# Bounded row gathers and spare blocks shared among the experts in a four-layer kernel

## The reference

```
router_logits = x @ gate_weight.T                       # 2048 x 32
top8 of softmax(router_logits), weights normalised
sec  -> the most similar of the 4 first choices, where the similarity is 0.5 or more
combine[token, expert] = sum of the weights that went there
for each expert:  y += (silu(x @ Wg.T) * (x @ Wu.T)) @ Wd.T * combine[:, expert]
out = layernorm(x + y)
```

## Time and profile before

| | |
|---|---|
| median of 3 runs | 1618.41 us (1615.53 to 1619.59) |
| the profiled execution | 1623.95 us |
| its span, first to last instruction | 1622.1 us |
| PE, DVE, ACT, POOL busy | 90%, 59%, 45%, 47% of the span |
| mean DMA rate | 166 GB/s |
| first gather issued | 961.55 us |
| last scatter issued | 1580.13 us |
| granted TensorE clock, mean | 0.957 |

### The profile page before, as it was taken

One profiled execution on the slowest core, in us unless ns is written; L12 is line 12 of the kernel. 1 busy time (PEld: TensorE's weight loads), 2 busy tenths in 40 slices (PEclk: granted clock), 3 DMA queues, 4 the chain that ended last, 5 costly groups with the idle time before them and its releaser, 6 DMA issues.

```text
span 1622.1 us, 33299 instructions
## 1 busy us (share of the span) xinstructions
PE 1454.7 (90%) x11189; PEld 822.8 (51%) x11190; DVE 954.9 (59%) x1869; ACT 726.1 (45%) x1313; POOL 767.6 (47%) x699
## 2 busy tenths in 40 slices
PE   3899999999999999999997369998899999999980
PEld 1566666544444444455444226665555666666650
DVE  6777777786757576635987864443333444444435
ACT  5344343455464646434444524443334444444433
POOL 2455454530010202134544445556567887776755
PEclk9999999999999999999998569999999999999995
DMA  6142111269776767421111547999988998888869
GB/s 236 58 126 90 41 26 39 68 234 316 232 259 226 259 227 259 167 95 53 55 43 44 184 151 198 254 268 255 273 238 176 168 170 156 148 150 148 149 91 317
DMA packets 97102, 269.52 MB, mean 166 GB/s; under 512 B 15152, under 2 KB 15568, under 8 KB 91920
## 3 DMA queue, kind: packets, MB, share of 16 engines
q1 hardware_dynamic: 61424, 182.75, 33.6%
q0 software_dynamic: 35616, 85.99, 27.5%
HBM read 158.83 MB, written 101.47 MB: 160 GB/s over the span
## 4 chain that ended last, share of the span: by engine, by line
PE 59%; DVE 15%; DMA 9%; issue 7%; POOL 5%; ACT 3%; SPq 1%; DVEq 0%; POOLq 0%; ACTq 0%
PE bank L870 16%; PE bank L891 8%; PE bank L552 8%; PE bank L684 6%; PE bank L690 6%; PE bank L713 6%; DMA acc<-X,WA 5%; PE bank L861 4%; DMA XT<-x_rows,WA 2%; ACT ARENA L1370 1%; POOL ARENA L1645 1%; PE bank L880 1%; POOL ARENA L1650 1%; DVE ARENA L1249 1%; DVE ARENA L1013 1%
## 5 line engine op out<-in xcount | busy, mean ns | idle before, releaser
L870 PE MATMUL bank<-ARENA,XT 128*128 x1908 | 366.4, 329 | 2.2 <-issue 1.1
L1778 POOL DMA_INDIRECT acc<-X,WA x159 | 252.8, 1590 | 130.3 <-DMA acc<-X,WA 53.3
L870 PEld LDWEIGHTS bank<-ARENA,XT 128*128 128x128 f16 x1908 | 181.2, 98 | 125.3 <-issue 8.1
L1334 DVE COPY XT<-bank 128x1024 f16<-128x1024 f16 x159 | 109.9, 691 | 204.5 <-PE bank L861 204.5
L1370 ACT ACTIVATE ARENA<-ARENA 128x512 f16<-128x512 f32 (+2 forms) x128 | 89.3, 709 | 249.0 <-DVE ARENA L1097 134.1
L891 PE MATMUL bank<-ARENA,XT 128*128 x795 | 198.3, 380 | 1.4 <-ACT XT L1370 1.0
L1772 POOL DMA_INDIRECT XT<-x_rows,WA x159 | 157.1, 988 | 87.0 <-DVE XT L1344 51.6
L1604 ACT ACTIVATE XT<-bank 128x192 f32<-128x192 f32 x159 | 52.7, 331 | 309.4 <-PE bank L870 309.4
L552 PE MATMUL bank<-WA,XT 128*128 128x512 f16 (+1 forms) x768 | 137.4, 333 | 24.1 <-DVE WA L933 19.8
L552 PE MATMUL bank<-XT,STG 128*128 128x512 f16 x640 | 151.9, 385 | 4.6 <-DVE ARENA L1143 4.3
L1632 POOL TENSOR_TENSOR rstd<-mv,mhalf 128x1 f32<-128x1 f32 x28 | 8.7, 310 | 255.8 <-DVE mv L939 255.8
(11 more groups left out here) (223 smaller groups left out, 2391.5 us busy)
## 6 DMA issues: line engine op xcount, KB each, us to landing
w_scratch<-WA SPq DMA_DIRECT2D x64, 640.0 KB, 3.9
ARENA<-w_scratch SPq DMA_DIRECT2D x32, 1280.0 KB, 7.4
ARENA<-w_exp SPq DMA_DIRECT2D x48, 640.0 KB, 5.2
WA<-w_exp SPq DMA_DIRECT2D x16, 640.0 KB, 5.2
ARENA<-ARENA SPq DMA_DIRECT2D x64, 128.0 KB, 2.3
acc<-ARENA SPq DMA_DIRECT2D x18, 256.0 KB, 3.0
x_rows<-ARENA SPq DMA_DIRECT2D x17, 256.0 KB, 2.6
STG<-xT SPq DMA_DIRECT2D x8, 512.0 KB, 4.4
```

The source lines that it names most:

```text
L870: mm = pe.matmul(d, xTb[k.u % 2][:, a * KD + kd, :], weights(sl, b, kd * 2 * DFF, 2 * DFF), start=(a, b, kd) == (0, 0, 0), stop=(a, b, kd) ...
L1334: dve.tensor_copy(xTb[k.u % 2].rearrange("p c n -> p (c n)"), bank[k.u % 2][:, :].bitcast(F16)).then_inc(xt_sb, 1)
L1778: pool.indirect_dma_start(acc[i % 2], bass.IndirectOffsetOnAxis(blkidx[:, i:i + 1], 0), yD[i % 8], None, compute_op=ALU.add).then_inc(y_ou ...
```

## The change

1. `x_rows` loses its 128 rows of zeros, and SP the two stores that filled them. The gather gets a bound, TOK - 1: rows whose number is above it are skipped, and the buffer keeps what it held there. So that a skipped row has no arbitrary combine weight in the first round, DVE clears the 8 x 32 weight columns of `xg` once. What a skipped row computes is added to the rows behind the last token, which nobody reads.
2. `spare` = the rounded value of (159 - 15.5 - all blocks needed) / 32 is added to the blocks of every expert. With 79 blocks needed it is (143.5 - 79) / 32 = 2.02, rounded 2: each expert has 2 blocks without tokens behind its own, and expert 31 has the 16 that remain as well. `ended`, `short` and `ends` follow. PE gets one more small matmul (the sum of `nb` for each expert), and DVE more small steps; `short` is now made after PE's sums instead of before.

```
-        xrows = nc.dram_tensor("x_rows", (ROWS, XROW), I32, kind="Internal").ap()
+        xrows = nc.dram_tensor("x_rows", (TOK, XROW), I32, kind="Internal").ap()
...
-            sp.dma_start(xrows[TOK:ROWS, 0:DIM], zeros.bitcast(I32)).then_inc(acc_init, 16)
-            sp.dma_start(xrows[TOK:ROWS, DIM:XROW], zeros[:, 0:EXPERTS].bitcast(I32)).then_inc(acc_init, 16)
...
             pe.matmul(bank[2][0:EXPERTS, 0:1], upper[0:EXPERTS, :], nb[0:EXPERTS, 0:1], start=True, stop=True)
+            pe.matmul(bank[2][0:EXPERTS, 1:2], ones[0:EXPERTS, 0:EXPERTS], nb[0:EXPERTS, 0:1], start=True, stop=True)
...
             choices(3)
+            own.did(dve.memset(xgs[:, :, DIM:XROW], 0.0))
             one_hots(2, 0, 12)
...
-            step(dve.tensor_scalar(nb[one, 0:1], cnt[one, :], MAGIC, None, ALU.subtract))
-            dve.tensor_scalar(short[one, :], nb[one, 0:1].to_broadcast([EXPERTS, P]), -float(EXPERTS), base[one, :],
-                              ALU.mult, ALU.add).then_inc(nb_ready, 1)
+            dve.tensor_scalar(nb[one, 0:1], cnt[one, :], MAGIC, None, ALU.subtract).then_inc(nb_ready, 1)
+            own.did(dve.tensor_scalar(pos1[one, :], iotap[one, :], 1.0, None, ALU.add))
             one_hots(2, 12, ROWS_B)
             places(3)
             dve.wait_ge(end_ready, 1)
-            step(dve.tensor_copy(endc[one, :], bank[2][one, 0:1]))
-            dve.tensor_scalar(ended[one, 0:NBLK], iotab[one, :], endc[one, :], None, ALU.is_ge).then_inc(ended_ready, 1)
-            own.did(dve.tensor_scalar(ends[0:1, :], bank[3][0:1, 0:EXPERTS], 1.0, None, ALU.add))
+            step(dve.tensor_scalar(spare[one, :], bank[2][one, 1:2], -1 / EXPERTS, (NBLK - 0.5 * (EXPERTS - 1)) / EXPERTS, ALU.mult, ALU.add))
+            step(dve.tensor_scalar(spare[one, :], spare[one, :], MAGIC, MAGIC, ALU.add, ALU.subtract))
+            own.did(dve.scalar_tensor_tensor(more[0:1, :], iota[0:1, :], 1.0, spare[0:1, :].to_broadcast([1, EXPERTS]), ALU.add, ALU.mult))
+            step(dve.scalar_tensor_tensor(endc[one, :], pos1[one, :], spare[one, :], bank[2][one, 0:1], ALU.mult, ALU.add))
+            own.did(dve.tensor_scalar(ended[one, 0:NBLK], iotab[one, :], endc[one, :], None, ALU.is_ge))
+            step(dve.tensor_scalar(cnt[one, :], nb[one, 0:1], spare[one, :], -float(EXPERTS), ALU.add, ALU.mult))
+            dve.tensor_scalar(short[one, :], cnt[one, :].to_broadcast([EXPERTS, P]), base[one, :], None, ALU.add).then_inc(ended_ready, 1)
+            own.did(dve.scalar_tensor_tensor(ends[0:1, :], more[0:1, :], 1.0, bank[3][0:1, 0:EXPERTS], ALU.add, ALU.add))
...
-                pool.indirect_dma_start(xg[i % NG], None, xrows, bass.IndirectOffsetOnAxis(blkidx[:, i:i + 1], 0)).then_inc(xg_in[i % NG], 16)
+                pool.indirect_dma_start(xg[i % NG], None, xrows, bass.IndirectOffsetOnAxis(blkidx[:, i:i + 1], 0),
+                                        bounds_check=TOK - 1, oob_is_err=False).then_inc(xg_in[i % NG], 16)
```

More of the change, by code:

```diff
@@ L206, in build @@
         cnt, nb, endc = r.take([1], F32), r.take([2], F16), r.take([1], F32)
+        spare, pos1, more = r.take([1], F32), r.take([1], F32), r.take([EXPERTS], F32)
         ended = r.take([160], F16)
@@ L231, in build @@
         r = Region(XT)
-        xg = [r.take([XROW], I32) for _ in range(NG)]
+        xgs = r.take([NG, XROW], F32)
+        xg = [xgs[:, i, :].bitcast(I32) for i in range(NG)]
         xTb = [r.take([2 * KD, P], F16) for _ in range(2)]
@@ L505, in _ @@
                 sp.wait_ge(xr_out[tt], 16 * BATCH)
-            sp.wait_ge(acc_init, 16 * (3 + ROWS // P + NT))
+            sp.wait_ge(acc_init, 16 * (1 + ROWS // P + NT))
             load_expert(4)
@@ L1783, in _ @@
                 pool.wait_ge(cw_out[j], 16 * BATCH // 2)
-            pool.wait_ge(acc_init, 16 * (3 + ROWS // P + NT))
+            pool.wait_ge(acc_init, 16 * (1 + ROWS // P + NT))
             for j in range(TB):
```

## The result

The changed kernel is faster by 0.6%: 1615.03 us, the median of 20 runs (1601.17 to 1623.74), against 1624.47 us for the kernel before in the same job (20 runs, 1615.53 to 1630.42). The ratio is 0.9939, 95% interval 0.9922 to 0.9957: 10 us gained, not 23.5.

The account below looks back on a forecast made before the run. PE bounds the kernel, except where scatters beside weight loads cost 24.7 us in the first 63 blocks; -24.7 + 1.0 (tables) + 0.2 (clearing weight columns) = -23.5 us from 1618.41 gives 1595 us, range 1589 to 1612.

Parts of the forecast that it names:

- The bound before: Expert stage, first 63 blocks: scatters landing slowly beside the burst of 24 weight loads cost PE 24.7 us, none after.
- Loads 16 us apart: Sign in the profile after: weight loads come about 16 us apart instead of every 10 us.
- Rival 3: Scatter landings depend on real rows, not loads; 1595 to 1600 us, counted with the forecast, together 70%.
- The tables: DVE between `places(3)` and the next one-hots: 8 steps for 3, 1.5 us for 0.50, so 1.0 us later.
- The gather on POOL: Bounded gather taken to stay at 0.99 us on POOL, no cost; a reading over 1.45 us would refute the prediction.
- Rival 1: The bound lengthens each gather and POOL becomes the bound: slower, 1679 us at twice the present gather; 12%.
- The spare blocks: Expert stage: 2 more blocks per expert space the loads, each expert comes out even, the whole 24.7 us is gained.
- The landing: Scatters in the crowded first stretch land after a median 8.0 us, so a block takes up to 4.08 us.
- The issue between landing and next scatter: Taken as about 0.15 us in the two-deep scatter chain: (8.0 + 0.15) / 2 = 4.08 us a block.
- The catching up: After each load POOL regains 0.46 us a block over 2.5 blocks, 1.15 us, against 0.9 us lost.
- By itself it is worth nothing on the path: Bounded gather in the expert stage: gain 0, since a gather is late only where a scatter holds POOL.
- rival 2: Only part is gained: POOL's gather grows about 0.5 us or the catching up fails; 1601 to 1611 us, 14%.

Follow-up runs that it names:

- e9: Kernel before, with each of the 24 later weight loads cut to 128 bytes a partition: 1597.72 us, ratio 0.9861 to the kernel before.
- e3: Changed kernel with the unbounded gather and rows of zeros put back, so only the spare blocks are shared out: 1632.82 us, ratio 1.0057 to the kernel before.
- e8: Changed kernel with each later load released by another semaphore, so issued one block later: 1619.06 us, ratio 0.9989 to the kernel before.
- e4: Changed kernel with `spare` set to 0, so only the bounded gather remains: 1616.86 us, ratio 0.9978 to the kernel before.
- e11: Changed kernel with each load cut in 4 DMAs issued at once, no wait between: 1598.63 us, ratio 0.9872 to the kernel before.
- e13: Kernel before with each load cut in 4 DMAs issued at once, no wait between: 1610.50 us, ratio 0.9927 to the kernel before.
- e15: e8 with each load cut in 4 DMAs issued at once: 1599.40 us, ratio 0.9856 to the kernel before.
- e5: Changed kernel with each later load cut in 4 parts, one at a time, one released by each block: 1598.61 us, ratio 0.9862 to the kernel before.
- e7: Kernel before with each load in 4 parts, one at a time; spare blocks and bound unchanged: 1745.97 us, ratio 1.0778 to the kernel before.
- e14: e3 with each load cut in 4 DMAs issued at once: 1605.96 us, ratio 0.9897 to the kernel before.

## Why the prediction was wrong

**Right.** The bound before: the loads in the burst cost 24.7 us by the prediction, 25.4 us of PE's loss in the trace, 0.3 us of it left without their bytes (e9). Where: a landing of a scatter follows a landing. Loads 16 us apart: 16.6 us on average from 993 to 1374 us, though not evenly (18.2 us at first, then mostly 14.6). PE's pace with and without tokens alike (e9). SP waits more for PE (206.2 us, 56.5 before) than for landings (143.8 us), but those have not gone. Rival 3 false.

The tables: DVE's chain starts and ends at

```profile
941.45 0.15 DVE L1298 TENSOR_SCALAR WA<-bank 32x1 f32<-32x1 f32 x1
...
942.81 0.17 DVE L1305 SCALAR_TENSOR_TENSOR WA<-WA,bank 1x32 int32<-1x32 f32 x1
942.91 2.92 DVE L1250 TENSOR_SCALAR STG<-WA 128x512 f16<-128x512 f16 x8
```

```profile
948.89 8.04 PE L793 MATMUL bank<-STG 128*128 128x512 f16 x24 [2.01 <-DVE STG L1250]
```

1.46 us for 0.50, against 1.5 forecast. The first gather stands at 960.74 us, 0.8 us earlier than before: a step of DVE ahead of the tables (L1213, before L1212) stands at 925.60 us for 927.27, 1.7 us earlier in this execution, and from there to the first gather it is 35.14 us instead of 34.28, 0.9 us for the 1.2 forecast.

The gather on POOL: 1.05 us for 0.99, far from the 1.45 us named as the limit; a pair takes 3.25 us (3.19 before) and stays under PE's 3.64. Rival 1 false. A skipped row is not nothing. A gather's packet holds two rows: before, there are 10176 packets of 4352 bytes (168 ns at the median); now there are 4090 of these, 6073 of 8 bytes for two skipped rows (about 10 ns) and 13 mixed ones. So the skipped rows leave no packet out, they make it short. Bytes of the software queue fall from 86 to 59.6 MB and its share of the engines from 27.5% to 22.8%.

**The step that failed** is the price of one load in "The spare blocks": "that is 2 blocks and 0.9 us behind", "it catches up ... 1.15 us in all", "so it comes out even within each expert", and from it "I take the whole 24.7 us as gained". Measured, one load leaves POOL's chain behind by 1.2 us on average after the catching up (PE's loss of 9.5 us and 18.9 us of lateness at block 107, over 24 loads), and 2.0 us with full gathers (49.0 / 24 in e3). Its three terms against the runs:

- *The landing.* 8.0 us was a median in a crowd, and of 28 of the 55 scatters only; over all 55 it is 7.5 us. A scatter that meets a load head-on mostly lands after 9 to 10 us (9.73 above; 10.27 in e3), and the one behind it after 6 to 8 (up to 9.5 in e3).
- *The issue between landing and next scatter.* The prediction took "about 0.15" us. Its own rows had 0.73, and after, from 1241.22 + 9.73 = 1250.95 to 1251.72, it is 0.77 us. That alone moves (L + x) / 2 by 0.3 us a block; with it, 8.0 us means 4.38 us a block, not 4.08. That 4.08 equalled the pace was taken as proof; it was chance. The pace of 4.07 is a mean of blocks at PE's own pace and, from block 30 to 59, of blocks at 3.64 + 19.3 / 29 = 4.31 us; and the landing taken was too long by about what the issue was too short. POOL's lateness says the same: 21.7 us at block 30 is 0.7 us a block, not 0.43.
- *The catching up.* (3.64 - 3.25) x 2.5 blocks = 1.0 us for each expert, nearly the 1.15 forecast, but against a head-on landing: 10.50 - 7.29 = 3.2 us. The mean of 4.5 blocks hides that most experts after block 30 have 4; 2 blocks are then left for the catching up, 0.8 us.

With those, each load costs 3.2 us or less depending on position, and gives back 1.0. **Not an average over the load's 8.2 us but the position of a scatter relative to its issue sets the cost**; no step of the prediction asked for that, and e8 shows that shifting the issue alone is worth 0.5%. Once the balance is negative, the cushion of 20 us is used up once, wherever the loads stand, and spreading them only makes the time longer in which it stays used up: that is e3.

**"By itself it is worth nothing on the path"**, of the bounded gather, was wrong too where it counts. Without it the change loses 0.6%; with it, it gains 0.6%. The prediction looked for the gather's own landing and POOL's time, and passed over in half a sentence ("it leaves more room to loads and scatters") that gathers share the DMA engines with the load and the scatter that collide. In the old order it is worth 0.2% (e4, whose interval ends at 1.0000).

So rival 2 is what happened: the "0.25 us an expert" by which the catching up was to hold did not hold, and its estimate, 12 us lost again over 24 loads, leaves 11 us of gain where 10 were measured. Its half about the gather on POOL did not happen; its half about the catching up did.

Of the 20 us between forecast and measured median, 14 are that step. The other 6 are the yardstick: the kernel before, at 1618.41 us in three runs, has a median of 1624.47 us in the job with the changed kernel.

**What stays open.** Why the changed kernel's loads slip from the cheap to the costly position was not tried by itself. In this execution it begins well before block 59: the scatter after the load at 1066.10 us lands after 7.9 us, the load at 1084.32 us falls 1.2 us after a scatter (8.4 us), the one at 1098.89 us 0.09 us after one (9.5 us). The next loads fall between scatters again, and from 1193 us on each meets one. That POOL's small lateness moves a scatter onto the load, and that the shorter time between loads after block 30 leaves less to catch up, fits this, but both are argued. Whether shorter packets or the start spread over 1.5 us make e11 and e13 to e15 faster is open. And the gain in the profiled executions (12.4 us of PE's loss less, of 14.1 us in all) is more than the medians' 9.4, since the profiled run is one of the faster ones.

## What to carry to other kernels

Before a burst of loads is spread out, price one load by what it does to the queue that binds: delay behind it less what the queue catches up before the next. If that is not clearly below zero, spreading lengthens the bad stretch instead of ending it. Take the price from a single collision in the order of time (the issue gap included), not from the median of a crowded stretch; and where a large load and small, latency-bound transfers share the DMA engines, try first to cut the load in four DMAs issued at once: that was worth 0.7 to 1.6% in all four variants here. With the change, e5 (0.9862), e11 (0.9872) and e15 (0.9856) cannot be told apart. The form of e5, one part at a time, leaves POOL the least late but keeps SP waiting; where a load was needed every 10 us (e7), it cost 7.8%.

## What the runs showed of the hardware

- A scatter that adds 256 KB lands after 5.1 us beside gathers and no load (e9), and after 8 us or more, up to 10.8, in 58 of 60 cases when it is issued from 1.4 us before to 1.0 us after a load of 1280 KB; issued 1.6 to 1.8 us before the load, it took 4.4 to 4.6 us at the first five loads of the changed kernel.
- The same 1280 KB in four DMAs, all issued within 2 us, brings slow scatters from 23 to 10 (e8 to e15), from 18 to 11 (changed to e11) and from 22 to 14 (before to e13), but only from 34 to 33 beside full gathers (e3 to e14).
- Two skipped rows of an indirect gather still cost a packet of 8 bytes (10 ns), and POOL takes 0.06 us more for each gather of 128 rows with a bound, 60% of them skipped on average.
- The DMA share of a stretch did not rank the kernels: 0.97 (e13) and 0.90 (e5) lost less than 0.78 (e8, 1220 to 1400 us).
